# One subtraction on VectorE and one exponential on ScalarE per attention round of the second image

## The chip, the core and the metric

The kernel runs on one core of one Trainium2 chip. TensorE (PE, with its weight loads as PEld) multiplies matrices into the PSUM banks, VectorE (DVE), ScalarE (ACT) and GpSimd (POOL) do the elementwise work, and SyncE (SP) issues DMAs. The engines run side by side, each one works through its own instructions in order, and they meet at semaphores. The time is that of the device for one execution, in microseconds; lower is better. The median of the runs shown is what counts.

## What is computed

Two images of 32x32 tokens with 128 channels go through three layers. The first is an attention of 8 heads in which each token sees the 7x7 tokens around it, with a bias for each relative position; its output is projected, gated, added to the input and normalised. The second is an additive attention over the 1024 tokens of each image, `softmax(tanh(q_i + k_j + bh) . Wa)`. The third sends each token to one of 8 experts. The change touches the softmax of the first layer:

```python
attn = jnp.einsum('bijnd,bijnpqd->bijnpq', q, kn)
attn = attn + bias[None]
a = jax.nn.softmax(attn.reshape(B, H, W, NH, K * K), axis=-1)
out = jnp.einsum('bijnpq,bijnpqd->bijnd', a, vn).reshape(B, H, W, C)
```

## The kernel before

**Rounds.** The local attention is worked off in 32 rounds, two for each block of 128 query tokens (4 image rows), one for the even and one for the odd heads. A round `rho` has four groups `g` (heads `2g + rho % 2`), each with the scores of 128 queries against the keys near them: 190 columns, or 133 in the four rounds at the top and the bottom of an image. Rounds 0 to 15 are the first image, and they run alone, before everything else. Rounds 16 to 31, those of the second image, are woven into the second layer's loop.

**One round of the second image.** TensorE writes the scores of two groups (`score_pair`, L801), and VectorE's `bias_score` (L1439) adds the bias table, negates, writes 128x190 into `prob[rho % 3]` in SBUF and leaves the row's minimum in a column of `mn[rho % 3]`. ScalarE's `soften` (L1243) takes `exp(mn - p)`, one ACTIVATE for each group, with the minimum as its bias. TensorE transposes the result in two chunks (L821, into bank 4), VectorE copies each chunk out (`turned_late`, L1468), and TensorE multiplies by the values (L848). After two rounds follow `heads_out_late` (L1518), the sums' inverse (L1484, L1471), a spread by TensorE (L904), scaling, projection (L919) and the gate (L1505). Layer norm rows of the second image are worked off on VectorE and GpSimd in between.

**The loop.** The second layer runs in 128 units `t`; units 0 to 63 are the first image. A unit's sums q + k of four 1024-wide tiles lie in one of four buffers of `front` (`ring[t % 4]`). GpSimd makes most of them (L654: two tiles of 1024 and two halves of 512 in units up to 35, two of 1024 and one of 512 later), VectorE the rest (L1630). ScalarE then takes the tanh in place, 4096 columns at a time (L1315); in units 36 to 63 it makes one tile itself (L1303) and takes 3072. TensorE sums the result against `Wa` in 16 matmuls of 512 columns (L1012) and frees the buffer (`h_used`), for which the sums of four units later wait. After every 8 units a block of queries ends: VectorE takes the least energies (L1654), ScalarE the exponential (L1333), TensorE transposes (L1038, also into bank 4), VectorE copies (L1662), TensorE attends (L1049), and VectorE and GpSimd (L662) norm and route the block.

**What sets the order.** Nothing is scheduled by a tool: each engine's loop over `t` lists what it does in step `t`, and a dictionary gives each round the step in which it begins: `BEGIN = dict(zip(range(RS, NR), [2, 4] + [6 + 3 * k for k in range(12)] + [42, 44]))`. For a round that begins at step b, VectorE biases two groups in step b and two in step b + 1; ScalarE softens two behind the tanh of unit b + 2 and two behind that of unit b + 3; TensorE transposes chunk 0 in step b + 4 and chunk 1 in step b + 5. Since a round begins every three steps, VectorE's copy of chunk 0 of one round stands in the same step b + 1, right behind the second bias pair of the next. Bank 4 takes all transposes in turn, and each waits until VectorE has copied out the one before (`turn_copied`); bank 7 takes all the small products, and each waits for VectorE to have read the one before (`misc_read`).

## Time and profile before

| | us |
|---|---|
| runs | 656.24, 653.71, 654.01 (median 654.01) |
| profiled execution | 650.61, of which the span is 648.8 |
| busy: PE, DVE, ACT, POOL | 520.2, 463.6, 559.7, 484.6 |

The profiled execution is 3.4 us shorter than the median, and 1.8 us of it lie outside the span. The page puts the span in 40 slices of 16.2 us. ScalarE is busy for nine tenths or more of every slice from about 97 to 567 us: this is the second layer's loop, with the second image's rounds in its first part, from about 100 to 290 us. In that part TensorE and GpSimd are near nine tenths too, and VectorE between seven and eight tenths. A busy share tells how full an engine is, not whether anyone waits for it; that is told by the waits, which name the engine that waited, and the one whose work ended its wait. "DVEq" or "issue" stand for a queue that had nothing to run that the profile shows.

### The profile page before, as it was taken

The page shows a single profiled execution, that of the slowest core. Times are in us where ns is not written, and L with a number is a line of the kernel's source. Part 1 is how long each engine was busy: PE and PEld are TensorE (multiplying, and loading weights), DVE is VectorE, ACT ScalarE, POOL GpSimd, SP SyncE. Part 2 cuts the span into 40 slices and gives each one's busy share as a digit, 9 for nine tenths or more (in the row PEclk, how much of TensorE's full clock was granted, in tenths as well). Part 3 has the DMA queues.
Part 4 walks back from the last instruction along what each step waited for, and adds up shares of the span by engine and source line. Part 5 has one row for each costly group of instructions (what it writes and reads, how often), then busy time and mean ns, then how long its engine had stood idle before and what let it go on. Part 6 is the DMA issues. An engine that isn't in the chain of part 4 may idle for free.

```text
span 648.8 us, 13483 instructions
## 1 busy us (share of the span) xinstructions
PE 520.2 (80%) x5069; PEld 258.5 (40%) x5069; DVE 463.6 (71%) x1372; ACT 559.7 (86%) x407; POOL 484.6 (75%) x582
## 2 busy tenths in 40 slices
PE   9998889997988898797787866676686767777993
PEld 7665543353435244343322312222231212335872
DVE  4777357777787967766678987787869787844465
ACT  3665399999999999999999999999999999971540
POOL 1006679987989898979989997979888887931385
PEclk9999699998989899998988999999989998988998
DMA  9500000000000000006200000000000000001400
GB/s 300 187 3 4 2 1 1 2 6 1 12 5 10 6 11 5 11 6 255 120 2 13 14 2 14 1 14 10 5 9 6 14 0 14 2 14 47 134 24 33
DMA packets 14480, 21.28 MB, mean 33 GB/s; under 512 B 1280, under 2 KB 12066, under 8 KB 14032
## 3 DMA queue, kind: packets, MB, share of 16 engines
q1 hardware_dynamic: 13008, 17.52, 8.1%
q0 software_dynamic: 1408, 2.91, 1.3%
q8 instruction: 40, 0.66, 0.4%
q14 instruction: 24, 0.20, 0.1%
HBM read 13.68 MB, written 7.37 MB: 32 GB/s over the span
## 4 chain that ended last, share of the span: by engine, by line
PE 35%; issue 21%; ACT 19%; DVE 19%; POOL 4%; DMA 1%; DVEq 0%; POOLq 0%; SPq 0%; ACTq 0%
ACT front L1315 17%; PE ps L1012 11%; DVE front L1630 5%; PE ps L821 3%; PE ps L1197 3%; PE ps L1201 2%; PE ps L848 2%; PE ps L1049 2%; POOL front L654 2%; PE ps L801 2%; PE ps L758 1%; PE ps L919 1%; DVE back L1439 1%; DVE back L1468 1%; PE ps L940 1%
## 5 line engine op out<-in xcount | busy, mean ns | idle before, releaser
L654 POOL TENSOR_SCALAR front<-k,q 128x1024 f32<-128x1024 f32 (+1 forms) x424 | 387.1, 931 | 45.3 <-PE ps L1012 33.8
L1315 ACT ACTIVATE front<-front 128x4096 f32<-128x4096 f32 (+1 forms) x125 | 418.5, 3394 | 2.2 <-POOL front L654 1.7
L1012 PE MATMUL ps<-front,cst 128*32 128x512 f32 x2032 | 257.7, 628 | 71.2 <-ACT front L1315 64.2
L1630 DVE TENSOR_SCALAR front<-ps,q 128x512 f32<-128x512 f32 x218 | 188.2, 901 | 25.6 <-PE ps L1012 21.9
L1012 PEld LDWEIGHTS ps<-front,cst 128*32 128x32 f32 x2032 | 55.8, 113 | 186.9 <-issue 96.7
L1243 ACT ACTIVATE back<-back,mn 128x190 f32<-128x190 f32 (+1 forms) x128 | 48.9, 433 | 14.4 <-DVE mn L1439 14.4
L821 PE MATMUL ps<-cst,back 128*114 128x128 f32 (+2 forms) x256 | 40.0, 286 | 11.2 <-DVE ptm L1662 5.8
L1303 ACT ACTIVATE front<-k,q 128x1024 f32<-128x1024 f32 (+1 forms) x50 | 46.0, 953 | 3.0 <-DVE k L1741 3.0
L1662 DVE COPY ptm<-ps 128x512 f32<-128x512 f32 x31 | 21.4, 691 | 37.6 <-PE ps L1038 35.8
L1439 DVE CUSTOM_DVE_ANT_0 back<-ps,back 128x190 f32<-128x190 f32 (+1 forms) x128 | 36.8, 334 | 3.5 <-PE ps L801 2.1
L601 POOL TENSOR_TENSOR lnw<-lny,lnh 128x4 f32<-128x4 f32 (+1 forms) x9 | 1.8, 197 | 48.8 <-DVEq L1605 45.8
L821 PEld LDWEIGHTS ps<-cst,back 128*114 128x114 f32 (+2 forms) x256 | 27.6, 131 | 17.4 <-issue 6.0
L1049 PEld LDWEIGHTS ps<-x_one,ptm 128*128 128x128 f32 x256 | 29.8, 191 | 8.4 <-issue 7.0
L1049 PE MATMUL ps<-x_one,ptm 128*128 128x129 f32 x256 | 32.5, 279 | 0.2 <-DVE ptm L1662 0.2
L662 POOL TENSOR_SCALAR rec<-rec,mv,sy 128x128 f32<-128x128 f32 x16 | 12.6, 786 | 25.9 <-DVEq L1689 25.9
L1372 ACT ACTIVATE front<-ps,cst 128x320 f32<-128x320 f32 x32 | 16.6, 527 | 16.3 <-PE ps L1197 16.1
L672 POOL DMA_INDIRECT xbuf<-rec,slots x16 | 17.4, 1086 | 14.7 <-DVEq L1724 11.6
L1468 DVE COPY back<-ps 114x512 f32<-114x512 f32 (+2 forms) x32 | 21.8, 682 | 8.9 <-PE ps L821 8.7
L848 PE MATMUL ps<-back,conv 76*32 76x64 f32 (+2 forms) x1024 | 25.3, 229 | 3.5 <-issue 2.2
L801 PE MATMUL ps<-conv 32*64 32x190 f32 (+1 forms) x512 | 26.4, 339 | 1.1 <-DVE mn L1439 0.9
L723 POOL DMA_INDIRECT out<-front,dest x20 | 20.6, 1031 | 7.3 <-issue 5.1
L1038 PEld LDWEIGHTS ps<-cst,pm 128*128 128x128 f32 x128 | 14.2, 147 | 28.1 <-issue 17.6
(162 smaller groups left out, 634.7 us busy)
## 6 DMA issues: line engine op xcount, KB each, us to landing
back<-in_w SPq DMA_DIRECT2D x2, 2048.0 KB
xbuf<-rec SPq DMA_DIRECT2D x1, 2720.0 KB, 14.1
back<-in_b SPq DMA_DIRECT2D x1, 1280.0 KB, 15.1
xT<-in_xT SPq DMA_DIRECT2D x4, 304.0 KB, 6.6
out<-rec SPq DMA_DIRECT2D x16, 64.0 KB, 1.5
back<-in_inner SPq DMA_DIRECT2D x1, 760.0 KB, 8.9
front<-xbuf SPq DMA_DIRECT2D x2, 360.0 KB, 4.3
front<-xbuf SPq DMA_DIRECT2D x1, 720.0 KB, 7.9
```

The lines of the kernel that those rows point to most:

```text
L654: last = nc.gpsimd.tensor_scalar(ring[u % DEPTH][:, at + lo:at + hi], k4[:, img * L + k0 + lo:img * L + k0 + hi], q4[:, m:m + 1], 1.0, ALU ...
L801: last = nc.tensor.matmul(bank(to, 0, n)[half * HQ:(half + 1) * HQ, :], q_par[r][dims, q0:q0 + HQ], kT[dims, k0:k0 + n], start=True, stop= ...
L821: last = nc.tensor.transpose(bank(to, g * P, (g + 1) * P)[0:hi - lo, :], prob[rho % 3][:, g, lo:hi], c_("ident"))
L848: last = nc.tensor.matmul(out[g * HP:(g + 1) * HP, :, half * HW:(half + 1) * HW], vals[0:hi - lo, value_block(j, c, half), 2 * g + r, :], ...
L1012: last = nc.tensor.matmul(bank(to)[c * U:(c + 1) * U, :], c_("wa", U - QPG - QPG * row, 2 * U - QPG - QPG * row), ring[t % DEPTH][:, at:at ...
L1049: last = nc.tensor.matmul(bank(6, 2 * P, 2 * P + C + 1), ptm[:, k, :], x_one[:, p // BPI * BPI + k, :], start=(k == 0), stop=(k == BPI - 1))
L1243: nc.scalar.activation(p, p, ACT.Exp, bias=mn[rho % 3][:, g:g + 1], scale=-1.0).then_inc(p_ready, 1)
L1303: last = nc.scalar.activation(ring[t % DEPTH][:, at:at + keys], k4[:, k0:k0 + keys], ACT.Tanh, bias=q4[:, m:m + 1])
L1315: last = nc.scalar.activation(ring[t % DEPTH][:, 0:to], ring[t % DEPTH][:, 0:to], ACT.Tanh)
L1439: nc.vector.tensor_tensor_reduce(out=prob[rho % 3][:, g, 0:n], in0=bank(frm, 0, n), in1=btab[kind][:, 2 * g + r, :], scale=-1.0, scalar=3e ...
L1468: nc.vector.tensor_copy(pts[rho % 2][0:hi - lo, c, :], bank(4)[0:hi - lo, :]).then_inc(turn_copied, 1)
L1630: last = nc.vector.tensor_scalar(ring[u % DEPTH][:, at + lo:at + keys], ps[:, base + k0 + lo:base + k0 + keys], q4[:, m:m + 1], None, ALU.add)
```

## The change

In the rounds of the second image, ScalarE's four exponentials (two in each of two steps) become one over all four groups' columns, in the later of the two steps, without a bias operand. VectorE gets a new instruction, `shift`: right behind the second bias pair it subtracts the four minima, each spread over its group's columns, from `prob[rho % 3]` in place, 4 x 190 (or 4 x 133) columns. It waits for its own four minima, and a new semaphore `shifted` tells ScalarE. The rounds of the first image are as they were.

```diff
-        pair_done = sem("pair_done")
+        pair_done, shifted = sem("pair_done"), sem("shifted")
...
+            def soften_all(rho):
+                act.wait_ge(shifted, rho - RS + 1)
+                p = prob[rho % 3][:, :, 0:KEYS[kind_of(rho // 2)]]
+                nc.scalar.activation(p, p, ACT.Exp, scale=-1.0).then_inc(p_ready, NG)
...
-                rho = round_at(t - 2, begin)
-                if rho is not None:
-                    soften(rho, (0, 1))
                 rho = round_at(t - 3, begin)
                 if rho is not None:
-                    soften(rho, (2, 3))
+                    soften_all(rho)
...
+            def shift(rho):
+
+                n = KEYS[kind_of(rho // 2)]
+                p = prob[rho % 3][:, :, 0:n]
+                dve.wait_ge(n_ready, NG * (rho + 1))
+                nc.vector.tensor_tensor(p, p, mn[rho % 3][:, :, None].broadcast_to([P, NG, n]),
+                                        ALU.subtract).then_inc(shifted, 1)
...
                 rho = round_at(t - 1, begin)
                 if rho is not None:
                     bias_pair(rho, 1)
+                    shift(rho)
```

VectorE's instructions around round 22 (it begins at step 18), before; `ISA` is the biasing instruction L1439 and the read of its minimum:

```order
L1662 COPY ptm<-ps 128x512
L1630 TENSOR_SCALAR front<-ps,q 128x512 x2
L1439 ISA back,mn<-ps,back 128x190
L1439 ISA mn 128x1
L1439 ISA back,mn<-ps,back 128x190
L1439 ISA mn 128x1
L1468 COPY back<-ps 76x512
L1662 COPY ptm<-ps 128x512
```

The same place after the change, in which VectorE's lines have moved on by two in front of the new function and by ten behind it (`prob` lies in `back`):

```order
L1672 COPY ptm<-ps 128x512
L1640 TENSOR_SCALAR front<-ps,q 128x512 x2
L1441 ISA back,mn<-ps,back 128x190
L1441 ISA mn 128x1
L1441 ISA back,mn<-ps,back 128x190
L1441 ISA mn 128x1
L1461 TENSOR_TENSOR back<-back,mn 128x760
L1478 COPY back<-ps 76x512
L1672 COPY ptm<-ps 128x512
```

The new instruction stands between the second bias pair and the copy of round 21's chunk 0. ScalarE's instructions from unit 25 to unit 30, round 24 (step 24) and the first pair of round 25 among them, before:

```order
L1315 ACTIVATE front<-front 128x4096 x2
L1333 ACTIVATE pm<-pm,nmin 128x1024
L1243 ACTIVATE back<-back,mn 128x190 x2
L1315 ACTIVATE front<-front 128x4096
L1243 ACTIVATE back<-back,mn 128x190 x2
L1315 ACTIVATE front<-front 128x4096 x2
L1243 ACTIVATE back<-back,mn 128x190 x2
L1315 ACTIVATE front<-front 128x4096
```

And after:

```order
L1320 ACTIVATE front<-front 128x4096 x2
L1338 ACTIVATE pm<-pm,nmin 128x1024
L1320 ACTIVATE front<-front 128x4096
L1249 ACTIVATE back<-back 128x760
L1320 ACTIVATE front<-front 128x4096 x3
```

The pair in the earlier step is gone, and in the later step one instruction stands in the place of two. TensorE, GpSimd and SyncE run the same instructions as before.

## Rows read from the trace of the kernel before

**Rows 1.** The page's groups: line, engine, operation, shapes, count | busy us, mean ns | idle.

```profile
L1315 ACT ACTIVATE front<-front 128x4096 f32<-128x4096 f32 (+1 forms) x125 | 418.5, 3394 | 2.2 <-POOL front L654 1.7
```

**Rows 2.** ScalarE in time order: start us, length us, line, operation, shapes, count.

```profile
145.06 3.61 ACT L1315 ACTIVATE front<-front 128x4096 f32<-128x4096 f32 x1
148.57 0.78 ACT L1243 ACTIVATE back<-back,mn 128x190 f32<-128x190 f32 x2
149.26 7.11 ACT L1315 ACTIVATE front<-front 128x4096 f32<-128x4096 f32 x2
```

**Rows 3.** Groups by shape: ScalarE's tanh and exponential, VectorE's additions.

```profile
L1315 ACT ACTIVATE front<-front 128x4096 f32<-128x4096 f32 x94 | 333.1, 3604 | 0.0
L1315 ACT ACTIVATE front<-front 128x3072 f32<-128x3072 f32 x31 | 85.5, 2758 | 2.2 <-POOL front L654 1.7 <-DVE front L1630 0.3
L1902 DVE TENSOR_TENSOR front<-front 128x384 f32<-128x384 f32 x3 | 1.7, 558 | 0.3
L1902 DVE TENSOR_TENSOR front<-front 128x256 f32<-128x256 f32 x4 | 1.7, 425 | 0.4
```

**Rows 4.** TensorE's waits (who for whom: total us, times, longest), 103 to 150 us.

```profile
PE ps L1012 <- ACT front L1315: 3.9, 6, 1.2
```

**Rows 5.** TensorE's waits, 153 to 362 us.

```profile
PE ps L1012 <- DVE nmin L1654: 6.8, 4, 2.2
PE ps L821 <- DVE ptm L1662: 5.8, 5, 3.5
PE ps L821 <- DVEq L1806: 4.4, 3, 2.0
```

**Rows 6.** TensorE in time order, unit 15 and behind it.

```profile
148.72 1.92 PE L1012 MATMUL ps<-front,cst 128*32 128x512 f32 x16 [1.20 <-ACT front L1315]
154.82 1.05 PE L821 MATMUL ps<-cst,back 128*76 128x128 f32 x4 [1.97 <-DVEq L1806]
```

**Rows 7.** ScalarE's units 31 and 32, and TensorE's unit 32.

```profile
210.82 7.13 ACT L1315 ACTIVATE front<-front 128x4096 f32<-128x4096 f32 x2
223.01 3.46 PE L1012 MATMUL ps<-front,cst 128*32 128x512 f32 x16 [2.11 <-DVE nmin L1654]
```

**Rows 8.** Rounds 22, 23 and 26: VectorE's work, TensorE's waits, ScalarE's pair.

```profile
168.73 0.68 DVE L1468 COPY back<-ps 76x512 f32<-76x512 f32 x1
169.48 0.42 PEld L1038 LDWEIGHTS ps<-cst,pm 128*128 128x128 f32 x4 [0.84 <-DVE back L1468]
...
181.12 0.42 DVE L1471 COPY rzx<-ps 128x256 f32<-128x256 f32 x1
181.77 0.20 PEld L904 LDWEIGHTS ps<-cst,rzx 128*128 128x128 f32 x2 [0.99 <-DVEq L1486]
...
220.25 0.65 PE L821 MATMUL ps<-cst,back 128*114 128x128 f32 x4 [0.95 <-DVE back L1468]
222.03 0.80 ACT L1243 ACTIVATE back<-back,mn 128x190 f32<-128x190 f32 x2
```

**Rows 9.** Round 28: VectorE's copy behind the bias.

```profile
245.69 0.69 DVE L1468 COPY back<-ps 76x512 f32<-76x512 f32 x1 [1.57 <-PE ps L821]
```

**Rows 10.** GpSimd's sums of 512 columns, 86 to 93 us: shortest, median, longest ns.

```profile
L654 POOL TENSOR_SCALAR front<-k,q x8: 683/689/962, 85.5 to 92.1; 128x512 f32<-128x512 f32 x8
```

**Rows 11.** VectorE and GpSimd around 88 us and 329 us, in time order.

```profile
88.46 0.42 DVE L1559 TENSOR_TENSOR y_all<-y_all,cst 128x256 f32<-128x256 f32 x1
92.88 0.60 DVE L1551 TENSOR_SCALAR x_one<-y_all,mvs,lny 128x128 f32<-128x128 f32 x2 [0.24 <-DVE lny L164]
...
329.33 0.77 DVE L1551 TENSOR_SCALAR x_one<-y_all,mvs,lny 128x128 f32<-128x128 f32 x1 [0.24 <-DVE lny L164]
327.15 3.97 POOL L654 TENSOR_SCALAR front<-k,q 128x1024 f32<-128x1024 f32 x4
```

**Rows 12.** Busy us of PE, PEld, DVE, ACT, POOL in two stretches; clock.

```profile
103.00:150.00 47.00, 43.00 (x486) 19.17 (x482) 35.98 (x96) 47.00 (x35) 43.84 (x53) 1.00 0.01 3
153.00:290.00 137.00, 118.32 (x1295) 54.34 (x1299) 104.88 (x352) 137.00 (x95) 117.47 (x130) 0.95 0.03 8
```

## The prediction, made before the changed kernel ran

> **What bounds the kernel now.** I read the page's groups first, then the waits and the order in time of the second layer's loop. ScalarE's tanh waits for 2.2 us in the whole run [rows 1], and ScalarE is busy for all 47 and all 137 us of the two stretches in which the rounds of the second image lie [rows 12]. So it looks as if each microsecond taken from ScalarE were one gained. The waits of TensorE say otherwise, and here the reader should look at who is named. From 103 to 150 us (units 5 to 15, rounds 16 to 20) TensorE waits for ScalarE's tanh six times, 3.9 us in sum [rows 4], and at unit 15 it starts its 16 matmuls at 148.72, when the tanh has ended at 145.06 + 3.61 = 148.67 [rows 2, 6]. There ScalarE leads. From 153 to 362 us TensorE's own waits name VectorE: 6.8, 5.8 and 4.4 us are the largest [rows 5]. At unit 32 the tanh has ended at 210.82 + 7.13 = 217.95, and TensorE begins that unit at 223.01, 5.1 us late, after a wait for VectorE [rows 7]. From unit 16 to about unit 66 TensorE is always behind ScalarE. It frees the four buffers late, GpSimd and VectorE fill them late, and ScalarE is busy only because the lead that it had is being used up; near units 50 and 66 nothing is left of it, and there it waits (the 2.2 us). The end of this stretch is therefore set by a loop of TensorE and VectorE, in which each waits for the other: the sums, the bias, the copies out of bank 4 and bank 7 against the transposes and small products. Behind unit 67, where no rounds are left, ScalarE leads again, and what was gained or lost by then stays.
>
> **What ScalarE saves.** Two exponentials of 190 columns move the next tanh by 149.26 - 148.57 = 0.69 us [rows 2], so a round takes 1.38 us of ScalarE. The new instruction has no bias operand, as the tanh has none, and that one costs 3604 ns at 4096 columns and 2758 ns at 3072: 0.826 ns a column [rows 3]. At 760 columns this gives 3604 - 3336 x 0.826 = 848 ns, less the 0.10 us by which two neighbours overlap (3.61 us long, but 3.51 to the next: 148.57 - 145.06) [rows 2]: 0.75. A round saves 0.63 us, the four rounds of 133 columns about the same by the same line, and sixteen save 10 us. Only what is saved while ScalarE leads reaches the end: five rounds, 3.1 us. TensorE has 3.9 us of waits there to give up [rows 4], so it can follow. The later 6.9 us make ScalarE wait instead.
>
> **What VectorE pays.** The subtraction is a tensor_tensor of 760 columns with both inputs in SBUF. The nearest rows are 425 ns at 256 columns and 558 ns at 384 [rows 3], 1.04 ns a column, so 558 + 376 x 1.04 = 949 ns, and 712 ns for 532 columns. It also waits for its own minima, which breaks the overlap with the instruction ahead (some 0.04 us of gap in place of 0.08 us of overlap, the end overlap coming back): I take 0.99 us more in VectorE's queue per round, 0.75 us for the narrow ones.
>
> To this comes GpSimd. A 512-column sum takes 689 ns, but the longest of eight took 962 ns [rows 10]; it began at 88.49, just as VectorE's 256-column tensor_tensor ran (88.46 to 88.88) [rows 11], and 0.27 us is the time of 256 columns. The other way round, VectorE's L1551 takes some 0.34 us alone (two in 0.60 us) and 0.77 us when GpSimd streams its sums [rows 11]. So each holds the other up. GpSimd is busy for 117.5 of 137 us [rows 12], mostly with sums of 0.7 or 1.1 us, so the subtraction will find one running about three times in four and wait some 0.47 us for its rest: 0.34 us a round. From below this wait is zero (the tensor_tensor at 88.46 shows little of it), from above a whole sum, 1.1 us. I take 1.33 us a round, 1.09 for a narrow one.
>
> The Trainium skill, in "SBUF — State Buffer", section "Who interferes with whom", has the same as a rule: a VectorE instruction with two SBUF inputs and a GpSimd instruction that reads SBUF shut each other out for the whole instruction, whoever comes first. The two cases in the rows agree with it; what it makes of GpSimd's time is the second rival below.
>
> **Who waits behind it.** In VectorE's queue the subtraction stands ahead of the copy of the last round's chunk 0, the inverse and its spread, or the layer norm rows. I looked at each of the sixteen places for what VectorE does next and for whom TensorE waits. In rounds 16 to 20, 24, 28 and 31 VectorE idles right behind the bias or soon after (1.57 us ahead of the copy in round 28 [rows 9]), or TensorE comes for the copy later: nothing, or nearly, is lost. In eight rounds (21, 22, 23, 25, 26, 27, 29 and 30) VectorE goes on at once and TensorE already stands waiting or comes within 0.2 us. In round 22 the copy ends at 169.41 and TensorE's transpose starts at 169.48 with a wait for it; in 23 the spread ends at 181.54 and TensorE's L904 follows at 181.77, 0.99 us idle; in 26 TensorE has waited 0.95 us for the copy [rows 8]; round 21 has the 1.97 us wait of [rows 6]. Those get later by what VectorE pays, less 1.3 us of slack in all (0.9 of it in round 30): 7 x 1.33 + 1.09 - 1.3 = 9.1 us. GpSimd's own loss, 0.79 us a round (760 x 1.04 ns), fits into the 19.5 us that it idles of 137 [rows 12]. ScalarE's own wait for `shifted` should cost nothing: where it comes closest, in round 26, its second pair starts at 222.03, and VectorE was through with the bias at about 219.5 (the copy of 0.68 us and then TensorE's start at 220.25 follow it) [rows 8], 2.5 us ahead.
>
> **Sum.** -3.1 + 9.1 = +6.0 us. Against the profiled execution that is 650.6 + 6.0 = 656.6; against the median of the runs, which is 3.4 us longer, 654.0 + 6.0 = 660.0 us. If VectorE never waits for GpSimd: 7 x 0.99 + 0.75 - 1.3 = 6.4, net +3.3, 657.3. If it waits for a whole sum each time: 7 x 2.05 + 1.8 - 1.3 = 14.9, net +11.8, 665.8.
>
> **Rivals.** (a) Faster. VectorE is busy for only 104.9 of 137 us [rows 12]; if its idle time takes up the subtraction, because the waits that I charge to its queue are in truth ends of TensorE's own work, ScalarE's chain carries through and the kernel gains 3.1 to 10 us: 646. It decides at the count of rounds that TensorE feels: at 1.33 us each, fewer than three of the eight, and the sign turns. Against it stand the waits of [rows 5, 8], for it the full ScalarE.
> (b) GpSimd becomes the bound early. In units 5 to 15 it is busy for 43.8 of 47 us [rows 12]; five rounds add 3 x 0.79 + 2 x 0.55 = 3.5 us (0.55 = 532 x 1.04 ns), and 47.3 us leave no room for ScalarE's 3.1 us gain, unless the lead that GpSimd builds up there is used. Then the +9.1 stands alone: 663. The rule of the Trainium skill named above ("SBUF — State Buffer") would lead here.
> (c) Half of it. If only four rounds are felt, 4 x 1.33 - 3.1 = +2.2, and if three, +0.9: about 656, no difference.
> (d) VectorE is passed over several times by GpSimd's queued sums, 2 us or more a round: 668 and above. In [rows 11] it got in after one.
>
> **Chances.** Forecast 0.43, (a) 0.19, (b) 0.12, (c) 0.22, (d) 0.04. About 0.5%, 3.3 us, is what a measurement of this kernel can tell from no change. Faster than 650.7: 0.19, all of (a). Within 650.7 to 657.3: (c) and 0.02 of the forecast's low edge, 0.24. Slower: the rest of the forecast, (b) and (d), 0.57. The range of 8 in 10 is 648 to 667: it leaves out the better half of (a) and (d).
>
> **What would show it.** In the changed profile, VectorE's L1461 should take about 0.95 us at its shortest and 1.3 us in the mean; GpSimd's 1024-column sums, now near 1.1 us, should show some of 1.9 us; ScalarE's L1249 0.85 us, with idle time of ScalarE near units 26 to 66 grown by more than 7 us, and TensorE's waits for VectorE from 153 to 290 us grown by some 9 us. TensorE should run earlier at unit 15 by about 3 us and later at unit 47 by about 6. If ScalarE still runs without gaps from 100 to 290 us and ends its rounds 10 us earlier, I am wrong and (a) holds. If L1461 takes 0.95 us throughout and GpSimd's sums keep their length, the holding up is wrong. If ScalarE already idles before unit 15, it is (b).

## The result, and the profile after

| | before | after |
|---|---|---|
| median of the runs, us | 655.03 (4 runs, 653.71 to 656.24) | 683.36 (4 runs, 681.22 to 687.12) |
| profiled execution: span, us | 648.8 | 679.6 |
| profiled execution: mean granted clock of TensorE | 0.948 | 0.932 |

The kernel became slower by the factor 1.0439 (95%: 1.0378 to 1.0500), 28.3 us. The prediction said 660.0 us and 648 to 667: slower was right, the size was not. Of all the runs of this document one, the 677.35 us of e11, fell in a slower state of the chip, and the ratios leave it out.

The page's groups of the kernel after (columns as in [rows 1]). Its first line answers to [rows 1], with ScalarE's tanh now at L1320; the last is the new subtraction:

```profile
L1320 ACT ACTIVATE front<-front 128x4096 f32<-128x4096 f32 (+1 forms) x125 | 418.6, 3401 | 24.5 <-POOL front L654 23.8
L654 POOL TENSOR_SCALAR front<-k,q 128x1024 f32<-128x1024 f32 (+1 forms) x424 | 396.0, 953 | 62.5 <-PE ps L1012 51.3
L1461 DVE TENSOR_TENSOR back<-back,mn 128x760 f32<-128x760 f32 (+1 forms) x16 | 34.4, 2150 | 0.6
```

The subtraction takes 2150 ns in the mean, where 950 ns of work had been reckoned and 1.3 us with its waits. ScalarE's tanh, which waited for 2.2 us in the whole run, now waits for 24.5. The view of the one line L1461 (count, then ns at the shortest, median and longest) shows that the mean is not what a round pays:

```profile
L1461 DVE TENSOR_TENSOR back<-back,mn x16: 712/1423/9762, 102.3 to 308.8; 128x760 f32<-128x760 f32 x12, 128x532 f32<-128x532 f32 x4
who waited for it (us, times):
  ACT back L1249: 15.0, 8
```

One took 9.76 us. It is round 19's. Here are VectorE, GpSimd, ScalarE and TensorE around it, each in time order (start us, length us, engine, line, operation, tiles, shapes, count, and in brackets the idle time before it with what ended it):

```profile
114.84 0.35 DVE L1441 CUSTOM_DVE_ANT_0 back<-ps,back 128x190 f32<-128x190 f32 x1
115.11 0.08 DVE L1441 DVE_READ_ACCUMULATOR2_ANT mn<- 128x1 f32 x1
115.23 1.91 DVE L1461 TENSOR_TENSOR back<-back,mn 128x760 f32<-128x760 f32 x1
...
128.02 0.08 DVE L1441 DVE_READ_ACCUMULATOR2_ANT mn<- 128x1 f32 x1
128.13 9.76 DVE L1461 TENSOR_TENSOR back<-back,mn 128x760 f32<-128x760 f32 x1
137.82 0.68 DVE L1478 COPY back<-ps 76x512 f32<-76x512 f32 x1
...
126.49 10.62 POOL L654 TENSOR_SCALAR front<-k,q 128x1024 f32<-128x1024 f32 x12
145.06 3.56 POOL L654 TENSOR_SCALAR front<-k,q 128x1024 f32<-128x1024 f32 x4 [7.96 <-PE ps L1012]
...
137.99 0.84 ACT L1249 ACTIVATE back<-back 128x760 f32<-128x760 f32 x1 [2.40 <-DVE back L1461]
...
128.04 1.92 PE L1012 MATMUL ps<-front,cst 128*32 128x512 f32 x16
138.64 1.08 PE L1038 MATMUL ps<-cst,pm 128*128 128x128 f32 x4 [8.68 <-DVE back L1478]
```

Read it from the GpSimd line. GpSimd works off twelve sums back to back from 126.49 to 137.11, and none of them is lengthened: the 1024-column ones take 1.13 to 1.14 us each, the 512-column ones 0.70 to 0.71. The subtraction, issued at 128.13 during the second, does not get in at the end of that one, nor of the next nine. It ends at 137.89, which is 0.79 us behind GpSimd's last sum (not rounded, 0.793), and 0.79 us is what 760 columns take at the 1.04 ns each of the prediction. So it got in when GpSimd had nothing left. And GpSimd had nothing left only because the kernel had stopped. The copy L1478 is queued behind the subtraction, TensorE waits 8.68 us for that copy, no unit is summed up meanwhile, and no buffer comes free (GpSimd's next sum waits 7.96 us for TensorE's L1012). In round 25 it was passed over at five ends of sums, and got in at the sixth, 4.77 us after its issue, though GpSimd had the next sum at hand:

```profile
221.76 5.57 DVE L1461 TENSOR_TENSOR back<-back,mn 128x760 f32<-128x760 f32 x1
227.25 0.68 DVE L1478 COPY back<-ps 76x512 f32<-76x512 f32 x1
...
220.13 7.75 POOL L654 TENSOR_SCALAR front<-k,q 128x1024 f32<-128x1024 f32 x8
```

Round 18, at 115.23, is what I had reckoned as the worst case of one round: it waited for one sum and took 1.91 us. Apart from rounds 19 and 25, the fourteen other subtractions took between 0.71 and 1.91 us. Sixteen without any wait would take 14.2 us (the first experiment below shows it), so 20.2 of the 34.4 us are waiting, and 13.4 of these lie in two rounds (9.76 + 5.57 - 2 x 0.95).

The table of stretches, with columns as in [rows 12], of the kernel before and, below the dots, after; the second stretch of before is in [rows 12]:

```profile
103.00:153.00 50.00, 45.76 (x511) 20.83 (x503) 38.98 (x105) 50.00 (x36) 46.84 (x57) 1.00 0.01 3
...
103.00:153.00 50.00, 38.96 (x410) 18.81 (x406) 44.30 (x83) 44.15 (x20) 41.72 (x48) 0.90 0.00 1
153.00:290.00 137.00, 106.34 (x1134) 48.88 (x1130) 111.50 (x310) 109.65 (x49) 110.28 (x116) 0.91 0.02 6
```

In the first 50 us TensorE was busy for 6.8 us less, and in the next 137 us for another 12.0 less, at a granted clock of 0.90 and 0.91 in place of 1.00 and 0.95. ScalarE's busy time in the second stretch fell by 27 us. About 7 us of that are the shorter exponentials (in e2 below, which has them without the subtraction, ScalarE is busy for 130.2 us there); the rest is work that had not been reached.

### The profile page after: what moved, and what is told of

The parts are those of the page before. It is cut to its first block, busy times and chain, and to the rows that moved or that the text cites. A ratio compares the mean times of both kernels' runs of the same rounds, so it can differ in the third digit from the quotient of the medians.

```text
span 679.6 us, 13467 instructions
## 1 busy us (share of the span) xinstructions
PE 525.4 (77%) x5069; PEld 262.2 (39%) x5069; DVE 498.5 (73%) x1388; ACT 551.5 (81%) x359; POOL 494.8 (73%) x582
## 4 chain that ended last, share of the span: by engine, by line
PE 35%; issue 23%; DVE 21%; ACT 17%; POOL 2%; DVEq 0%; DMA 0%; POOLq 0%; another core or an unknown queue 0%; SPq 0%; ACTq 0%
ACT front L1320 15%; PE ps L1012 11%; DVE front L1640 6%; PE ps L821 3%; PE ps L848 3%; PE ps L1197 3%; PE ps L1049 2%; PE ps L1201 2%; PE ps L758 2%; DVE back L1441 1%; PE ps L801 1%; DVE back L1478 1%; PE ps L1038 1%; PE ps L919 1%; DVE ptm L1672 1%
## 5 line engine op out<-in xcount | busy, mean ns | idle before, releaser
L654 POOL TENSOR_SCALAR front<-k,q 128x1024 f32<-128x1024 f32 (+1 forms) x424 | 396.0, 953 | 62.5 <-PE ps L1012 51.3
L1320 ACT ACTIVATE front<-front 128x4096 f32<-128x4096 f32 (+1 forms) x125 | 418.6, 3401 | 24.5 <-POOL front L654 23.8
L1012 PE MATMUL ps<-front,cst 128*32 128x512 f32 x2032 | 259.3, 632 | 69.6 <-ACT front L1320 59.7
L1640 DVE TENSOR_SCALAR front<-ps,q 128x512 f32<-128x512 f32 x218 | 188.2, 901 | 23.2 <-PE ps L1012 18.9
L1012 PEld LDWEIGHTS ps<-front,cst 128*32 128x32 f32 x2032 | 56.0, 113 | 185.6 <-issue 101.0
L1243 ACT ACTIVATE back<-back,mn 128x190 f32<-128x190 f32 (+1 forms) x64 | 24.4, 432 | 14.4 <-DVE mn L1441 14.4
L1461 DVE TENSOR_TENSOR back<-back,mn 128x760 f32<-128x760 f32 (+1 forms) x16 | 34.4, 2150 | 0.6
L1049 PEld LDWEIGHTS ps<-x_one,ptm 128*128 128x128 f32 x256 | 31.2, 198 | 8.4 <-issue 7.0
L1038 PE MATMUL ps<-cst,pm 128*128 128x128 f32 x128 | 21.8, 295 | 10.5 <-DVE back L1478 10.4
```

The lines of the kernel that those rows point to most:

```text
L654: last = nc.gpsimd.tensor_scalar(ring[u % DEPTH][:, at + lo:at + hi], k4[:, img * L + k0 + lo:img * L + k0 + hi], q4[:, m:m + 1], 1.0, ALU ...
L1012: last = nc.tensor.matmul(bank(to)[c * U:(c + 1) * U, :], c_("wa", U - QPG - QPG * row, 2 * U - QPG - QPG * row), ring[t % DEPTH][:, at:at ...
L1038: last = nc.tensor.transpose(bank(to, k * P, (k + 1) * P), pm[:, (4 * half + k) * P:(4 * half + k + 1) * P], c_("ident"))
L1049: last = nc.tensor.matmul(bank(6, 2 * P, 2 * P + C + 1), ptm[:, k, :], x_one[:, p // BPI * BPI + k, :], start=(k == 0), stop=(k == BPI - 1))
L1320: last = nc.scalar.activation(ring[t % DEPTH][:, 0:to], ring[t % DEPTH][:, 0:to], ACT.Tanh)
L1461: nc.vector.tensor_tensor(p, p, mn[rho % 3][:, :, None].broadcast_to([P, NG, n]), ALU.subtract).then_inc(shifted, 1)
```

## The experiments

Each kernel was compared with the kernel before on the same chip. The ratio that stands behind a median comes from that comparison, with its 95% interval; it can differ by up to 0.002 from the quotient of the two medians. So e2 below is 2.4 us faster by its ratio and 1.6 us by the medians, and e1 10.0 us and 9.5 us slower; the expectations quote the smaller figures, the text the ratios. To see where in the run a microsecond goes, I took from each trace the time at which ScalarE starts the tanh of a unit, less that of the same unit in the kernel before (units 5, 16, 34, 50 and 67 start there at 103.5, 149.3, 222.7, 292.9 and 358.1 us). "Idle" is TensorE's idle time from 84 us to the end of its 66th group of 16 matmuls, and "slowed" what the groups that took over 2.3 us (as the 3.46 us of [rows 7]) took beyond 1.93 us; both are sums over the profiled run, in us.

```
kernel                  unit 5  unit 16  unit 34  unit 50  unit 67   idle  slowed
before                     0        0        0        0        0     40.7     9.1
after                    0.0     +4.0    +22.0    +29.9    +30.0     67.4     9.4
e2 no subtraction       +1.1     -1.5     -1.4     -0.6     +0.5     38.7     9.1
e3 exponentials later   +1.0     +1.6     +1.7     +2.5     +2.6     40.5    12.5
e1 one SBUF input       -1.3     -4.0     +2.1    +10.2    +10.3     48.2    12.7
e9 the same, later      -0.5     -3.1     +3.5     +7.0     +8.2     45.4    11.8
e5 extra, one input     -1.2     -1.1     +4.8    +10.0    +13.2     50.5    11.8
e4 extra, two inputs    +0.3     +3.1    +21.7    +30.5    +31.5     65.7     9.6
e11 two inputs, later   -0.3     +0.3     +8.3    +12.2    +12.3     53.8    10.4
e7 two rounds old way   +2.0     +0.9     +9.7    +20.9    +24.1     52.3    15.8
e6 GpSimd chained       +1.1     +0.7    +10.8    +20.0    +19.8     52.6    14.7
e8 four pieces          +2.8     +4.7    +30.6    +45.5    +45.6     66.2    18.3
e10 less VectorE work   -0.1     -2.7     -4.4     +0.8     +1.7     40.2    10.0
```

Little is won or lost behind unit 67, as the prediction said: the spans of after and e1 differ from that of before by 30.8 and 11.0 us. Each row is one execution, and e3 tells how much that can mean. By its runs it is as fast as before, and yet its row ends at +2.6 with 3.4 us more of "slowed". So differences of this size between two rows are not told from chance.

**e1: the subtraction with one input in SBUF.** If the waits are GpSimd's doing, they go when the second operand does not come from SBUF. Against the kernel after:

```diff
-                nc.vector.tensor_tensor(p, p, mn[rho % 3][:, :, None].broadcast_to([P, NG, n]),
+                nc.vector.tensor_tensor(p, p, bank(5, 0, NG)[:, :, None].broadcast_to([P, NG, n]),
```

> The changed kernel, but the subtraction's second operand is four columns of PSUM bank 5 (keys that stay there, one value per row and group, so the softmax is the same) in place of the minima in SBUF: one SBUF input, the same 760 columns, the same place in VectorE's queue. Theory A, that the loss comes from VectorE and GpSimd shutting each other out: every subtraction takes 0.95 to 1.0 us, none of GpSimd's sums is longer than 1.15 us, and the time is 655 to 659 us. Theory B, that the loss comes from the place in VectorE's queue, whatever the operands: the time stays above 672 us.

Measured: 663.83 us, 1.0153 (1.0115 to 1.0191) of before. The line of the subtraction, and GpSimd's sums (ns at the shortest, median, longest), in this kernel, and below the dots the sums in the kernel after:

```profile
L1461 DVE TENSOR_TENSOR back<-back,ps x16: 707/946/947, 101.0 to 289.1; 128x760 f32<-128x760 f32 x12, 128x532 f32<-128x532 f32 x4
L654 POOL TENSOR_SCALAR front<-k,q x424: 681/1110/1191, 78.4 to 580.6; 128x512 f32<-128x512 f32 x123, 128x1024 f32<-128x1024 f32 x19
...
L654 POOL TENSOR_SCALAR front<-k,q x424: 681/1110/1833, 80.2 to 600.4; 128x512 f32<-128x512 f32 x123, 128x1024 f32<-128x1024 f32 x19
```

Same instruction, same place, same queue: 0.947 us at the longest, and GpSimd's longest sum falls from 1833 to 1191 ns. So the waits on both sides need the second SBUF input. They cost 1.0439 - 1.0153 = 0.0286 of the run, 18.7 us. But 10.0 us are still lost, where I had reckoned 3.3 for this very case; the time lies between what the two theories said.

**e2: no subtraction.** ScalarE takes `exp(-p)` directly; the softmax's shift is left out. VectorE still takes the minima, but nobody reads them. Against the kernel after:

```diff
-                act.wait_ge(shifted, rho - RS + 1)
+                act.wait_ge(n_ready, NG * (rho + 1))
...
-                    shift(rho)
```

> The changed kernel without the subtraction (the second image's softmax goes without its minimum, which it does not need for these values): ScalarE's saving alone, 10 us by the sum of the prediction. Theory A, that behind unit 15 a loop of TensorE and VectorE leads: only the first five rounds' 3.1 us come out, about 652 us, and ScalarE gets gaps between 150 and 290 us. Theory B, that ScalarE leads all through: 645 us.

Measured: 652.69 us, 0.9964 (0.9944 to 0.9984). ScalarE's half of the change, alone, gives 2.4 us. TensorE's waits from 103 to 362 us in this kernel, and below the dots ScalarE's from 103 to 290 us (who for whom: total us, times, longest):

```profile
PE ps L1012 <- DVE nmin L1664: 6.8, 4, 2.2
PE ps L821 <- DVE ptm L1672: 5.8, 5, 3.5
PE ps L821 <- DVEq L1816: 4.4, 3, 2.0
...
ACT front L1320 <- POOL front L654: 5.9, 4, 2.5
```

The three waits of TensorE for VectorE are those of [rows 5] to the digit (at lines moved by ten), while the 3.9 us of [rows 4] have shrunk to 0.6 (the view has two such waits in all), and ScalarE waits where it did not. Between unit 5 and unit 16 the tanh gains 2.6 us in this trace (and as much in that of e10 below), and between unit 34 and unit 67 it loses 2.0 of them again. The profiled execution, 654.22 us, is near the longest of this kernel's ten. This is the picture of the first paragraph of the prediction: ScalarE leads for ten units, then TensorE and VectorE do.

**e3: the four old exponentials, all in the later step.** The kernel before, with ScalarE's pairs put together in one step but not into one instruction:

```diff
-                rho = round_at(t - 2, begin)
-                if rho is not None:
-                    soften(rho, (0, 1))
                 rho = round_at(t - 3, begin)
                 if rho is not None:
-                    soften(rho, (2, 3))
+                    soften(rho, range(NG))
```

> The kernel before with all four exponentials of a round in the later of the two steps, nothing else: the move alone. Both theories: no difference, 655 us within 1; if TensorE in fact waited for the exponentials, 2 us or more slower.

Measured: 653.95 us, 0.9993 (0.9967 to 1.0019). Moving the first pair to a later step costs nothing that can be told.

**e4 and e5: the kernel before with a subtraction added.** Both leave ScalarE as it was, and put one more VectorE instruction where `shift` stands. It subtracts from a bias table into spare space, so its result is used by nobody. e4 takes both inputs from SBUF; e5 differs in the operand `bank(5, 0, NG)[:, :, None]` in PSUM alone.

```diff
+            def extra(rho):
+                n = KEYS[kind_of(rho // 2)]
+                spare = xT[:, 0:NG * KMAX].rearrange("p (g k) -> p g k", g=NG)
+                dve.wait_ge(n_ready, NG * (rho + 1))
+                nc.vector.tensor_tensor(spare[:, :, 0:n], btab[INNER][:, 0:NG, 0:n],
+                                        mn[rho % 3][:, :, None].broadcast_to([P, NG, n]), ALU.subtract)
...
                     bias_pair(rho, 1)
+                    extra(rho)
```

> The kernel before with ScalarE's work untouched, and in the subtraction's place on VectorE a subtraction of the same size whose result nobody reads (bias table less minima, both in SBUF, into a dead part of xT). Theory A, two costs on VectorE's side (being shut out by GpSimd's sums, and delaying what stands behind it) and little from ScalarE: 26 to 32 us slower than before, with at least one subtraction over 3 us. Theory B, the loss comes from ScalarE's one exponential being late and long: within 5 us of before.

> The same extra subtraction in the kernel before, but with its second operand in PSUM bank 5: one SBUF input. Theory A: 0.95 us each, 9 to 13 us slower than before, as with the changed kernel and this operand (9.5 us), plus the 1.6 us that ScalarE's saving was worth there. Theory B: within 3 us of before.

Measured: e4 682.03 us, 1.0412 (1.0388 to 1.0437); e5 668.85 us, 1.0229 (1.0188 to 1.0269). The added instruction in e4, and below the dots in e5:

```profile
L1458 DVE TENSOR_TENSOR xT<-back,mn x16: 712/1346/9639, 102.0 to 308.8; 128x760 f32<-128x760 f32 x12, 128x532 f32<-128x532 f32 x4
...
L1458 DVE TENSOR_TENSOR xT<-back,ps x16: 708/946/948, 100.5 to 288.9; 128x760 f32<-128x760 f32 x12, 128x532 f32<-128x532 f32 x4
```

Nobody waits for this subtraction's result, and e4 is, within the intervals, as slow as the whole change. So the loss is in VectorE's queue and not in ScalarE's wait for `shifted`, though that wait was there (15.0 us in eight rounds, where the prediction had said none). The two kernels differ by 0.0027 (1.8 us), which is known to some 4 us only, and that is also the room left for such a cost. The long one came back as well, in the same round and by the same pattern: in e4 VectorE issues it at 128.01, GpSimd works off thirteen sums without a stop until 136.85, and the subtraction ends at 137.65, 0.80 us later:

```profile
128.01 9.64 DVE L1458 TENSOR_TENSOR xT<-back,mn 128x760 f32<-128x760 f32 x1
125.57 11.28 POOL L654 TENSOR_SCALAR front<-k,q 128x512 f32<-128x512 f32 x13
```

e5 says what 14.2 us of VectorE's queue at this place cost without any waiting: 0.0229 x 654 = 15.0 us, where the expectation had 9 to 13. Its row shows where. From unit 5 to unit 16 nothing is lost (-1.2 to -1.1), as the prediction had it for rounds 16 to 20. The eleven later rounds, which have 9.9 us of these subtractions, cost 14.3 us up to unit 67. TensorE's idle time grows by 9.8 us and its slowed groups by 2.7; the second is no more than e3 shows without any loss. The stretch from 153 to 290 us in e5 (granted clock 0.93, where [rows 12] has 0.95):

```profile
153.00:290.00 137.00, 111.86 (x1202) 51.27 (x1203) 105.94 (x335) 129.67 (x92) 109.14 (x121) 0.93 0.02 7
```

**e9 and e11: the same subtraction at the end of VectorE's step.** `shift` moves from behind the second bias pair to behind everything else that VectorE does in the step, the copy of chunk 0 among it (the step's sums L1640 stand ahead of it in both places). e9 has e1's operand in PSUM, e11 the minima in SBUF. Against e1 and against the kernel after:

```diff
                     bias_pair(rho, 1)
-                    shift(rho)
...
                     dve.sem_inc(t_ready[3], 1)
+                rho = round_at(t - 1, begin)
+                if rho is not None:
+                    shift(rho)
```

> The changed kernel with the operand in PSUM and the subtraction at the end of its step in VectorE's queue, behind the copies and the small products' work, in place of right behind the second bias pair. Theory A, what stands behind it in the queue is what costs: most of the 9.5 us go, 654 to 658 us. Theory B, VectorE as a whole is full in these rounds, and any 0.95 us more costs the same wherever it stands: 662 to 665 us.

> The changed kernel as it is (minima in SBUF, two SBUF inputs) with the subtraction at the end of its step. Being shut out is not changed by the place: some subtractions still take 2 us and more. Theory A: the part of the loss that the waits behind it cause goes, 660 to 675 us. Theory B: 683 us as in the changed kernel.

Measured: e9 659.55 us, 1.0083 (1.0050 to 1.0117); e11 672.75 us, 1.0298 (1.0256 to 1.0341), its four runs from 664.54 to 677.35. The place is worth 0.0070 (4.6 us) in e9 against e1, and 0.0141 (9.2 us) in e11 against after. For e9 that is between the two theories: about half of the loss depends on what stands behind the subtraction. The place does not cure e11, whose profiled run, its fastest, still has one of 5.40 us:

```profile
143.36 5.40 DVE L1461 TENSOR_TENSOR back<-back,mn 128x760 f32<-128x760 f32 x1
```

The wide scatter of e11's runs would fit a wait that is long in some executions and not in others; only one of the four has a trace, so this is not shown.

**e7: rounds 19 and 25 the old way.** The two rounds with the long waits do without the subtraction and take the four exponentials with their bias.

```diff
+OLD = (19, 25)
...
-                act.wait_ge(shifted, rho - RS + 1)
+                if rho in OLD:
+                    return soften(rho, range(NG))
+                act.wait_ge(shifted, rho - RS + 1 - sum(o < rho for o in OLD))
...
-                    shift(rho)
+                    if rho not in OLD:
+                        shift(rho)
```

> The changed kernel with rounds 19 and 25 done in the old way on both engines (no subtraction, four exponentials with bias in the later step). These are the rounds in which the subtraction took 9.8 and 5.6 us. Theory A, these two long waits are felt in full: 13 us come back, 668 to 671 us. Theory B, being passed over is a matter of chance per subtraction and moves to other rounds when the timing moves: one or more of the others now takes over 4 us, and less than 8 us come back.

Measured: 677.64 us, 1.0364 (1.0325 to 1.0403). Taking away two subtractions with 13.4 us of waiting gave back 0.0075, 4.9 us. The remaining fourteen, and the stretch from 153 to 290 us in this kernel:

```profile
L1464 DVE TENSOR_TENSOR back<-back,mn x14: 712/1290/3626, 104.3 to 299.9; 128x760 f32<-128x760 f32 x10, 128x532 f32<-128x532 f32 x4
...
153.00:290.00 137.00, 113.42 (x1150) 51.66 (x1150) 107.03 (x320) 117.93 (x58) 113.66 (x119) 0.89 0.02 7
```

Another round now took 3.63 us (it had taken 1.08 in after, at 150.86), so the two rounds are no special places. The rows of the table show where the gain went. At unit 34, behind both rounds, e7 stands 12.3 us ahead of after, nearly all of the 13.4 us of waiting; at unit 67 only 5.9 us ahead. Up to there the two waits were felt nearly in full, and half of what was won without them was lost again by unit 67. In that profile TensorE's slowed groups took 15.8 us too long, against 9.4 in after, and its mean granted clock was 0.916 against 0.932. That the clock is what took the gain back is not shown: over all four runs each, the clocks are 0.914 to 0.919 and 0.910 to 0.932.

**e6: GpSimd with gaps between its sums.** In units 5 to 51 GpSimd waits for the end of each of its first two sums of a unit before it starts the next, so that VectorE finds a gap and not an overlapping seam. Against the kernel after:

```diff
                                                        1.0, ALU.add, ALU.mult)
+                        if 5 <= u < 52 and n < 2:
+                            chain(last)
+                if 5 <= u < 52:
+                    chain.end()
```

> The changed kernel, but in units 5 to 51 GpSimd waits for the end of each of its first two 1024-column sums before it starts the next, so that two of the four seams between its sums of a unit have a gap in place of an overlap of some 0.03 us; the rest is untouched. Theory A, VectorE is passed over only where GpSimd's next sum has already started before the last one ends: no subtraction takes over 3.5 us, and the time falls to 664 to 674 us (GpSimd itself loses 0.1 to 0.2 us at each such seam). Theory B, VectorE gets in by chance at any seam: one or more subtractions still take over 4 us, and the time stays above 676 us.

Measured: 667.08 us, 1.0201 (1.0167 to 1.0234), 15.6 us less than after, though GpSimd now stood idle for 0.09 us at each of the chained seams. The subtraction:

```profile
L1465 DVE TENSOR_TENSOR back<-back,mn x16: 711/983/1822, 104.8 to 298.6; 128x760 f32<-128x760 f32 x12, 128x532 f32<-128x532 f32 x4
```

None waits for more than one sum, and their total is 19.3 us in place of 34.4. But only eight of the sixteen got in at one of the gaps; four got in where two sums still overlap, and four had nothing to wait for (0.71 to 0.95 us).

**e8: the subtraction in four pieces of 190 columns.** Shorter instructions hold GpSimd up for less time; but each must get in for itself.

```diff
-                nc.vector.tensor_tensor(p, p, mn[rho % 3][:, :, None].broadcast_to([P, NG, n]),
-                                        ALU.subtract).then_inc(shifted, 1)
+                for g in range(NG):
+                    last = nc.vector.tensor_tensor(p[:, g, :], p[:, g, :], mn[rho % 3][:, g:g + 1].broadcast_to([P, n]),
+                                                   ALU.subtract)
+                last.then_inc(shifted, 1)
```

> The changed kernel with the subtraction in four instructions of 190 columns, one for each group. Theory A, each instruction with two SBUF inputs has to get in for itself: four waits in place of one, GpSimd's next sum between every two of them, the four together 4 us and more in most rounds, 700 us or more. Theory B, once VectorE is in, it stays in while its queue holds such work: within 3 us of the changed kernel's 683.

Measured: 694.47 us, 1.0639 (1.0591 to 1.0686), the slowest of all. The line of this kernel:

```profile
L1462 DVE TENSOR_TENSOR back<-back,mn x64: 283/484/2944, 106.6 to 326.7; 128x190 f32<-128x190 f32 x48, 128x133 f32<-128x133 f32 x16
```

A round's four pieces took from 1.3 to 4.7 us together, 38.1 us in all in place of 34.4, with several short waits in place of one. That is less than theory A said (4 us and more in one round only, not in most), and so was the time; it is also far from B's 683. The kernel lost 13 us more than after, of which 3.7 us are direct. TensorE's slowed groups took 8.9 us more than in after, and the granted clock was 0.903 to 0.911 in all four runs.

**e10: no subtraction, and less work on VectorE.** As in e2 the subtraction and the shift of the softmax are left out, and here the minimum is not taken either. The bias of two groups is added by one tensor_tensor with one input in PSUM, in place of two biasing instructions with their reads. Against the kernel before, beside e2's edits:

```diff
-                for g in range(2 * pair, 2 * pair + 2):
-                    bias_score(rho, g, 2 + g % 2)
...
+                table = btab[kind].rearrange("p (g r) k -> p g r k", r=2)[:, 2 * pair:2 * pair + 2, r, :]
+                scores = ps[:, 2 * 512:4 * 512].rearrange("p (b k) -> p b k", b=2)[:, :, 0:n]
+                nc.vector.tensor_tensor(prob[rho % 3][:, 2 * pair:2 * pair + 2, 0:n], scores, table,
+                                        ALU.add).then_inc(n_ready, 2)
```

> No subtraction and no minima at all in the second image's rounds: VectorE adds the bias of two groups in one tensor_tensor from PSUM (one SBUF input, 380 columns, some 0.55 us) in place of two instructions and two reads (1.2 us a round less some 0.9: 0.3 us a round), ScalarE takes one exponential per round. Theory A, behind unit 15 VectorE's queue is what TensorE waits for: what VectorE is spared comes out, 3 to 6 us faster than before, 649 to 652 us. Theory B, ScalarE's and TensorE's own work leads: no more than the 1.6 us of the kernel without the subtraction.

Measured: 650.30 us, 0.9957 (0.9933 to 0.9981), against 0.9964 (0.9944 to 0.9984) of e2: no difference between the two that can be told. So the time lies in theory A's range, but what VectorE was spared beyond e2 is not shown to have come out. The new instruction is short, and never held up:

```profile
L1462 DVE TENSOR_TENSOR back<-ps,back x32: 423/543/554, 99.9 to 279.0; 128x380 f32<-128x380 f32 x24, 128x266 f32<-128x266 f32 x8
```

These two are the only versions faster than the kernel before, by 0.4%, and both do it by leaving the minimum out of the exponential, which it guards against large scores.

## Why the direction was right and the size wrong

The three terms of the prediction, each against the runs that differ in it (the measured ones are differences of ratios times 654 us, uncertain by 1, 3 and 5 us in this order; their sum is the whole by construction):

| term | predicted | measured |
|---|---|---|
| ScalarE's saving | -3.1 | -2.4 (e2) |
| the subtraction in VectorE's queue, without waiting for GpSimd | +6.4 | +12.4 (e1 less e2) |
| waiting for GpSimd | +2.7 (at most +8.5) | +18.7 (after less e1) |
| sum | +6.0 | +28.7 |

The direction was right for the reason that the prediction gave, and not by luck: what ScalarE saves hardly comes out (e2), and what VectorE pays is more (e1, e4, e5).

The terms do not simply add up. A second pair for the waiting, e4 less e5, gives +12.0 us (uncertain by 3) where after less e1 gives +18.7.

**ScalarE's saving** was right, in its size and in its place. The exponential of 760 columns takes 830 ns (848 reckoned), the five rounds up to unit 15 gave 2.6 us, and the later rounds made ScalarE wait instead. Beside the subtraction its worth is not settled: e1 is 0.0076 (5.0 us) faster than e5, which differs from it in what ScalarE does, but after is no faster than e4.

**The bare time in the queue** was mis-sized by half, in the paragraph "Who waits behind it". The duration of 0.95 us was right to the digit (0.947). The price was not. That rounds 16 to 20 cost nothing held, in e1 (2.7 us gained from unit 5 to unit 16, and 2.6 in e2) and in e5. Of the eleven rounds behind them I had found eight felt, from gaps in the trace of before, at 6.4 us. Even all eleven at full length make only 9.9 us, and from unit 16 to unit 67 they cost 14.3 us in e5, and in e1 12.3 more than in e2. So every microsecond put into the queue there cost at least itself. The step took each round by itself, against the schedule as it stood. A reading that fits, and is not shown, is that TensorE comes a little later for everything once the first delay is in, and that the idle time that VectorE had behind the bias was in part the slack of the next step. I cannot divide the missing 6 us further: from e2 to e1 TensorE's idle time grows by 9.5 us, and the excess of its slowed groups by 3.6, which is no more than e3 shows without any loss. The move to the end of the step (e9) shows what part depends on who stands behind it: 4.6 us.

**The waiting for GpSimd** is where the prediction failed. The step is the sentence that bounds the wait from above by "a whole sum, 1.1 us". It held in fourteen of sixteen rounds, where nothing took over 1.91 us, and the wait was 0.48 us in the mean (0.34 reckoned; a sum was under way at every one of the sixteen, not at three in four). In the other two the subtraction waited for six and for eleven of GpSimd's sums to end. The single case that I had, L1551 in [rows 11], could not show more than one, and I took it for a rule: whoever comes next gets in next. It is also a tensor_scalar with one tensor as input, so it was not a case of the two SBUF inputs that the prediction counted it for. Rival (d), VectorE passed over several times, was the mechanism, given 0.04 and priced at 668. It was rare by rounds, but two rounds hold 13.4 of the 20.2 us of waiting, since such a wait can go on until the whole loop has stopped. How much of the 18.7 us those two make stays open: without them (e7) 4.9 us came back. And the other fourteen do not come cheap. e7 has 8.7 us of waiting left in its fourteen subtractions (21.0 us in all, 12.3 of them the bare time), and is 0.0211, 13.8 us, slower than e1. The Trainium skill, "SBUF — State Buffer", section "Who interferes with whom", describes the exclusive use of the shared ports, and e1 and e4 agree with it: two SBUF inputs are held up, one is not. It says that the one who issues second blocks until the first finishes. The trace differs here: the subtraction that came at 128.13 was still blocked when the sum then under way had finished, and ten more of GpSimd's, all of which started after 128.13, went ahead of it.

**The rivals.** (a), faster, fell: behind unit 16 ScalarE idles, with or without the subtraction (e2). (b), GpSimd as the bound, fell too: in the kernel after GpSimd is busy for only 41.7 of the 50 us from 103 to 153, and its sums wait for TensorE (51.3 us in the page's second line), not the other way round. Its fifteen lengthened instructions make 9.3 us over the whole loop. The sign that the prediction gave for (b), ScalarE idle before unit 15, did appear (5.8 us from 100 to 150), but 2.4 us of it is the wait for round 19's subtraction and 2.8 us follow on that stop. (c) fell with e5.

**What was to be seen.** L1461's shortest of 760 columns was 0.98 us (0.95 said), its mean 2.15 (1.3 said). Sums of 1.83 us appeared (1.9 said). The loop should have been 3 us earlier at unit 15; in e2 it was 2.6 earlier relative to unit 5, and in the kernel after the 9.76 us of round 19 lie in front of that point and hide it (+4.0). At unit 47 it should have been 6 us later; by unit 50 it was 29.9. One term of the upper bound was also too small by itself: a whole sum on top of 0.99 us makes 2.09 and not 2.05 us a round, 0.3 us in the sum.

**What stays open.** Why the same kind of seam between two of GpSimd's sums let VectorE in at once in some rounds and not in the others. Of the fourteen short ones, eleven got in where two sums overlap, two at a gap of 0.16 to 0.17 us ahead of another instruction of GpSimd's, and one did not wait. In the trace of the kernel after two neighbouring sums overlap by 0.014 to 0.046 us where it was passed over, and by 0.015 to 0.033 us where it was let in at once. That they overlap may be needed: with gaps (e6) no wait was longer than one sum. But e6 also shifts every time in the loop, only eight of its rounds met a gap, and at a rate of 7 in 62 sixteen rounds would be free of a long wait by chance about one time in seven (an estimate). Nor did I divide the 18.7 us into the direct waits of 20.2 us and what they set off. TensorE's clock is open as well: its mean was 0.932 to 0.951 over the runs of before, 0.910 to 0.932 over those of after and 0.903 to 0.911 over those of e8, and whether it makes part of the loss or only goes with it no run here separates. Which rounds were passed over is known for one execution of each kernel; after and e4 agree on rounds 19 and 25.

## What to carry to other kernels

Before a VectorE instruction with two SBUF inputs goes into a stretch in which GpSimd works from SBUF back to back, ask how long GpSimd goes on without a pause: the wait can last that long (9.76 us here), and the length of one of GpSimd's instructions does not bound it. One operand in PSUM took the wait away (0.95 us at the longest), and four short instructions were worse than one long one. And where engines wait for each other in a loop, count time added to the queue that the others wait for at its full price at least, until an added dummy of the same length says otherwise.

## What the runs showed of the hardware

- A VectorE tensor_tensor with both inputs in SBUF, issued while GpSimd worked off tensor_scalar instructions from SBUF, was passed over at ten ends of them in a row and took 9.76 us (9.64 us in another kernel). Over the kernels after, e4, e7 and e11, 7 of 62 such subtractions took more than 3.5 us; none did with the second operand in PSUM (48 of 48 at 0.95 us or less, in e1, e5 and e9).
- Where it waited, it ended its 760 columns 0.79 to 0.80 us after the end of the GpSimd instruction behind which it got in (0.83 where it had come only 0.15 us ahead of that end), while e1's takes 0.95 us: the waiting hides its start.
- GpSimd's instruction behind an admitted subtraction is longer by about the time of those columns: up to 1.83 us in place of 1.11 at 1024 columns, 1.37 to 1.39 in place of 0.69 at 512.
- The bias of two groups added by one 380-column tensor_tensor out of PSUM, without the minimum, takes 543 ns (e10), where two instructions of 190 columns with their reads take 0.63 us (127.47 to 128.10 in the kernel after).
